# An embedding, attention and mixture-of-experts kernel on one core: V fetched in smaller pieces and partly later, first score loads ahead of a meeting, experts' tokens in three groups instead of five

## What is computed

```python
def _L0_attn_ref(x, w_qkv, b_qkv, w_proj, b_proj):
    y = x @ fq_weight(w_qkv).T + b_qkv
    y, _ = fq_act(y)                       # 8 bits, one scale for all of q, k and v
    q, k, v = ...                          # 64 sequences of 68 tokens, 12 heads of 16
    attn = jnp.einsum('bhnd,bhmd->bhnm', q, k) * attn_scale
    attn, s_attn = fq_act(attn)            # one scale for all scores
    attn = int_log_softmax(attn, s_attn)
    o = jnp.einsum('bhnm,bhmd->bhnd', attn, v)
    o, _ = fq_act(o)
    o = o @ fq_weight(w_proj).T + b_proj
    o, _ = fq_act(o)
    return o

def _L0_ffn_ref(x, w_fc_sh, w_proj_sh, w1, w2, router_w, balance_bias):
    shared = _mlp(x, w_fc_sh, w_proj_sh)
    scores = jax.nn.sigmoid(xf.astype(jnp.float32) @ router_w.T)
    _, idx = jax.lax.top_k(scores + balance_bias, K)        # 2 of 8 experts
    tw = jnp.take_along_axis(scores, idx, axis=-1)
    tw = tw / (tw.sum(-1, keepdims=True) + 1e-20)
    ...
    return shared + routed.reshape(Bx, Tx, Cx)

h = concatenate(patches of the images @ W, text embedding MLP)   # 64 x 68 tokens, 192 wide
h = h + _L0_attn_ref(_layernorm(h), ...)
h = h + _L0_ffn_ref(_layernorm(h), ...)
```

## Time and profile before

| What | Value |
|---|---|
| median of 3 runs | 942.96 us (940.64 to 943.77) |
| the profiled execution's own time | 945.13 us |
| its span | 943.2 us |
| DVE, PE, ACT, POOL busy | 709.8, 604.6, 515.3, 252.1 us |
| mean granted TensorE clock | 0.709 |
| DMA | 92.77 MB, mean 98 GB/s |

### The profile page before, as it was taken

One profiled execution on the slowest core, in us unless ns is written; L12 is line 12 of the kernel. 1 busy time (PEld: TensorE's weight loads), 2 busy tenths in 40 slices (PEclk: granted clock), 3 DMA queues, 4 the chain that ended last, 5 costly groups with the idle time before them and its releaser, 6 DMA issues.

```text
span 943.2 us, 19819 instructions
## 1 busy us (share of the span) xinstructions
PE 604.6 (64%) x6474; PEld 451.9 (48%) x6474; DVE 709.8 (75%) x1831; ACT 515.3 (55%) x951; POOL 252.1 (27%) x245
## 2 busy tenths in 40 slices
PE   3589889898406667058888888341222349999970
PEld 2589768776204334024555555331112237777760
DVE  2535668777548999789999999987776788667783
ACT  3122268766345424048888888454554226888840
POOL 2022111120011221012222222110355750036575
PEclk9999789999755555555565555555555569999985
DMA  7974024443222221022222222451011241467753
GB/s 172 258 202 120 18 54 131 109 119 120 96 66 82 68 68 51 9 47 33 43 43 43 43 43 37 106 220 59 33 55 58 77 147 51 140 188 218 226 168 113
DMA packets 151481, 92.77 MB, mean 98 GB/s; under 512 B 88828, under 2 KB 143684, under 8 KB 151084
## 3 DMA queue, kind: packets, MB, share of 16 engines
q1 hardware_dynamic: 143560, 72.28, 29.3%
q0 software_dynamic: 7856, 19.68, 7.2%
HBM read 45.62 MB, written 31.85 MB: 82 GB/s over the span
## 4 chain that ended last, share of the span: by engine, by line
DVE 28%; PE 24%; issue 17%; SPq 16%; ACT 9%; DMA 3%; POOL 2%; POOLq 0%; DVEq 0%; ACTq 0%
PE ps L1844 19%; SPq L659 8%; ACT R L806 5%; ACT R L809 3%; DVE M L1413 3%; DVE M L1414 3%; SPq L637 2%; POOL R L799 2%; SPq L636 2%; SPq L638 2%; DVE R L1403 2%; DVE R L1801 1%; PE ps L2018 1%; PE ps L2114 1%; PE ps L1869 1%
## 5 line engine op out<-in xcount | busy, mean ns | idle before, releaser
L1844 PE MATMUL ps<-R 128*128 128x256 f16 (+9 forms) x2064 | 310.2, 303 | 53.0 <-DVE R L1801 16.1
L1844 PEld LDWEIGHTS ps<-R 128*128 128x128 f16 (+5 forms) x2064 | 221.6, 129 | 113.3 <-issue 59.1
L806 ACT ACTIVATE R<-ps 128x768 f16<-128x768 f16 (+7 forms) x257 | 159.8, 649 | 93.5 <-PE ps L2018 18.9
L1844 PE MATMUL ps<-M 32*128 32x68 bf16 (+4 forms) x1196 | 100.6, 242 | 117.5 <-DMA M<-R 67.2
L1844 PEld LDWEIGHTS ps<-M 32*128 32x128 bf16 (+3 forms) x1196 | 64.9, 115 | 168.9 <-issue 66.5
L809 ACT ACTIVATE R<-R,sc 128x512 f16<-128x512 f32 (+7 forms) x107 | 83.6, 838 | 105.6 <-DVE R L1403 40.1
L799 POOL DMA_INDIRECT R<-y_by_tile,M x68 | 66.7, 981 | 98.0 <-DMA y_by_tile<-R 79.4
L771 POOL TENSOR_TENSOR R<-R,M 128x884 f32<-128x884 f32 x32 | 53.2, 1664 | 145.5 <-ACT M L958 145.5
L790 POOL DMA_INDIRECT x_by_expert<-R,M x68 | 67.2, 989 | 60.3 <-DVEq L1707 40.5
L806 ACT ACTIVATE R<-R 128x512 f16<-128x512 f32 (+4 forms) x121 | 64.1, 549 | 35.3 <-DVE R L1801 34.5
L2018 PE MATMUL ps<-ident_b,R 128*68 128x128 bf16 x416 | 53.8, 298 | 25.3 <-ACT R L806 23.9
(11 more groups left out here) (293 smaller groups left out, 1050.2 us busy)
## 6 DMA issues: line engine op xcount, KB each, us to landing
R<-x_by_expert SPq DMA_DIRECT2D x41, 192.0 KB, 2.6
y_by_tile<-R SPq DMA_DIRECT2D x41, 192.0 KB, 2.3
R<-in_x_dram SPq DMA_DIRECT2D x12, 576.0 KB, 9.0
M<-R SPq DMA_DIRECT2D x16, 260.0 KB, 2.3
M<-R SPq DMA_DIRECT2D x32, 130.0 KB, 2.0
R<-w_split SPq DMA_DIRECT2D x1, 4032.0 KB, 23.1
R<-h_rows SPq DMA_DIRECT2D x1, 3264.0 KB, 14.3
out_dram<-R SPq DMA_DIRECT2D x17, 192.0 KB
```

The costliest lines, as they stand in the source:

```text
L806: return act.activation(out_, in_, ACT.Copy)
L1844: return pe.matmul(o, a, b, start=start, stop=stop, skip_group_check=True)
```

## The change

Four groups of edits:

1. **V.** `V_LOADS` keeps only sequences 6 to 32, in five pieces of 4 or 6 sequences; the loads of 32 to 48 and 0 to 6 at step 26 and of 48 to 64 at the end are gone from SP's list. Ten pieces (`V_LATE`) are issued by ACT after the meeting, two after each of the chunks 1 to 5. The rounding of V into `VQ` moves from DVE to POOL, in the list ahead of POOL's reduction of the score extremes; `spread_v` waits for it by a new semaphore.
2. **Constants.** Five DVE instructions (`output_constants`) move from just ahead of the second meeting to chunk 1 of the first pass.
3. **Ahead of a meeting.** `barrier` takes a function that is called between the engine's sign-in and its wait: SP issues the staging loads of groups 0 and 1 and PE the scores of group 0 there at the second meeting; SP issues `load_rest` there at the third.
4. **Experts.** Windows of 5, 7 and 5 pairs instead of 2, 4, 5, 4, 2; `SHARED_FIRST` 10 instead of 12; `READY` becomes 17, 31, 41; combines 1.5 steps apart instead of 2. DVE normalises (`normal`) instead of ACT; the root is `Sqrt` and the score `Sigmoid` instead of `Ln` and `Exp`; `weigh` is part of `choose` again; the order of DVE's and ACT's lists is regular.

```diff
-WINDOWS = [(0, 2), (2, 6), (6, 11), (11, 15), (15, 17)]
-SHARED_FIRST = 12
+WINDOWS = [(0, 5), (5, 12), (12, 17)]
+SHARED_FIRST = 10
-        def barrier(eng, name):
+        def barrier(eng, name, ahead=None):
             eng.drain().then_inc(sem("all_engines_done"), 1)
+            if ahead:
+                ahead()
             eng.wait_ge(sem("all_engines_done"), 5 * n)
-        V_LOADS = [(20, 11, 24, 32), (24, 12, 6, 24), (26, 6, 32, 48), (26, 6, 0, 6), (None, 15, 48, B)]
+        V_LOADS = [(20, 11, 24, 28), (20, 11, 28, 32), (24, 12, 6, 12), (24, 12, 12, 18), (24, 12, 18, 24)]
+        V_LATE = [(1, 0, 4), (1, 4, 6), (2, 32, 36), (2, 36, 40), (3, 40, 44), (3, 44, 48), (4, 48, 52), (4, 52, 56), (5, 56, 60), (6, 60, B)]
-            COMBINE_AT.append(max(free, COMBINE_AT[-1] + 2 if i else 0))
+            COMBINE_AT.append(max(free, COMBINE_AT[-1] + 1.5 if i else 0))
...
-            sp.wait_ge(sem("qkv_extremes"), 16)
-            load_v(48, B, 15)
+                sp.wait_ge(sem(f"v_saved{a}"), v_stores(16 + a))
+                sp.wait_ge(sem(f"w_stored{a}"), 16 * sum(WCH_DMAS[a::2]))
...
+            def load_ahead():
+                for g in range(2):
+                    wait(sp, "scored", 32 + g - 1)
+                    load_seqs(g, slice(g * 2, g * 2 + 2), 2)
-            barrier(sp, "sp")
+            barrier(sp, "sp", load_ahead)
...
-            pipeline(sp, [(load_two, 0), (spread_v, 4), (load_rest, 4)], 32)
-            barrier(sp, "sp")
+            pipeline(sp, [(load_two, 0), (spread_v, 4)], 32)
+            barrier(sp, "sp", load_rest)
...
+            pool.wait_ge(sem("v_added"), 2)
+            pool.tensor_scalar(VQ, vt, sc[0:N, Q_CAPM:Q_CAPM + 1], H16 + 512.0, ALU.min, ALU.subtract).then_inc(sem("v_whole"), 1)
             reduce_pair(A_MX, "a_minmax")
...
             for c in range(8):
                 to_halves(c)
+                for at, first, end in V_LATE:
+                    if c == at:
+                        act.dma_start(yv[:, first:end, :], v_dram[:, first:end, :]).then_inc(sem("v_in"), 16)
...
-                chain(act, "scalar_step", act.activation(rs2[:, 1, t], rs2[:, 0, t], ACT.Ln))
-                act.activation(rs2[:, 1, t], rs2[:, 1, t], ACT.Exp, scale=0.5).then_inc(sem("ln2_sqrt"), 1)
+                act.activation(rs2[:, 1, t], rs2[:, 0, t], ACT.Sqrt).then_inc(sem("ln2_sqrt"), 1)
...
+            def output_constants():
+                for k, (lo, hi) in enumerate(((C1, C1 + 3), (C1 + 1, P), (C1 + 2, P))):
+                    ch(dve.tensor_reduce(bmask[:, k:k + 1], ident[:, lo:hi], X, ALU.add, negate=k > 0))
+                ch(dve.reciprocal(vrow, prow))
+                ch(tt(bprow, bprow, vrow, ALU.mult))
...
-            dve.wait_ge(sem("v_added"), 2)
-            ts(VQ, vt, s1(Q_CAPM, N), H16 + 512.0, ALU.min, ALU.subtract)
...
+            def normal(i):
+                wait(dve, "rows2", i - 1)
+                for j in range(2):
+                    n = 2 * i + j
+                    last = ts(xf[:, i % 2, j, :], hf[:, n, :], mv2[:, n, 0:1], rs2[:, 2, n:n + 1], ALU.subtract, ALU.mult)
+                last.then_inc(sem("xf"), 1)
...
+            residuals(0, 5)
             variances(0)
+            residuals(5, 7)
             deviations(0)
+            normals(0)
+            residuals(7, 9)
             choose(0)
+            residuals(9, 11)
             place(0)
+            residuals(11, 12)
             variances(1)
...
+            def scores_ahead():
+                pe.wait_ge(sem("st_qk0"), 9 * 48)
+                pe.wait_ge(sem("extremes"), 31)
+                scores(0, 0, 0, 0, 1)
...
-            barrier(pe, "pe")
+            barrier(pe, "pe", scores_ahead)
```

More of the change, by code:

```diff
@@ L614, in _ @@
                     if s == at:
-                        if end == 48:
-                            for a in range(2):
-                                sp.wait_ge(sem(f"w_stored{a}"), 16 * sum(WCH_DMAS[a::2]))
-                        if first == 0:
-                            sp.wait_ge(sem("h_out"), 16 + 4 * GRID)
-                        load_v(first, end, UNIT_ORDER.index(unit) if unit < 15 else 15)
+                        load_v(first, end, UNIT_ORDER.index(unit))
                 if s - 2 in WSTEP:
@@ L1731, in make_table @@
                 ch(dve.memset(step_[:, 0, :], float(WB)))
[L1732 removed]
+                for w in range(3):
                     last = dve.memset(step_[:, 0, E * (w + 1) - 1:E * (w + 1)], -float((E - 1) * WB))
@@ L2099, in turn_window @@
                         route(i - 2)
-            for w in range(NW):
+            for w in range(3):
                 turn_window(w)
```

210 lines of the change are left out of this document (73 added, 137 removed).

## The result

The changed kernel takes **967.68 us** (median of 4 runs, 967.10 to 969.18) against 943.37 us (4 runs, 940.64 to 947.03) for the kernel before: a ratio of 1.0258 (1.0221 to 1.0295). It is slower by 24 us; I had forecast 16 us faster. The profiled execution of after took 969.18 us, its span is 967.4 us. Times are medians of a kernel's fast executions; one slow execution of e10 (2485 us) and one of e12 (1358 us) are left out.

What follows compares the result with a forecast made beforehand. Bounds: DVE's wait behind V fetches, its chain at the second meeting, SP's release at the third, POOL's indirect DMAs last. Terms -12.5 + 1.0 + 1.9 - 2.5 - 4.5 - 1.3 + 0.9 = -17.0 gave 928.1 or 926.0; forecast 927 us, range 918 to 938.

Steps and rivals of the forecast that it cites:

- It reads one tensor, so I take the copy: POOL's rounding of V: priced at a copy's 1.12 ns per element, 13.8 us; bounds memset 11.0, two-tensor product 23.1.
- V, rounded by POOL: Ahead of POOL's reduction at the second meeting: moving the rounding from DVE costs +1.9 us, ends -0.9 and +11.2.
- My rule for the point from which it decides: Second meeting: POOL's pass, started at 371.74, sets the reduction's start once it takes over 8.5 us.
- V, in the first pass: Ten late V pieces beside SP's staging copies: +1.0 us, bounds 0 to +3.8.
- The wait at the first meeting: End of the qkv stage: V fetches ahead of the stores make DVE's wait; moving them saves 12.5 us, bounds 0 to 12.5.
- Constants and scores ahead: Second meeting: constants moved into the first pass -2.5 us, first loads and scores issued before the meeting -4.5.
- the third meeting: POOL's reduction there no longer waits for SP's issuing: -1.3 us.
- Tiles and the longer run of gathers: Experts, first store to last gather: 31 tiles for the second group +5.3, 48 gathers instead of 44 +5.1, together +10.4 us.
- the combines' +1.5: Experts' end: combines 1.5 steps apart make DVE wait for gathers at each window's end, +1.5 us (0 to 3).
- The first store: Experts: the first tile's store moves from 803.31 to 792.3, -11.0 us, after earlier rows and PE's lowered clock.
- the first scatter: Experts: first window's rows ready at 680 instead of 666.12, about 14 us later; last scatter about 2 earlier.
- The rival on the other side: POOL's pass eats every gain from 30.8 us (2.5 ns per element) on; kernel slower, 943 to 950 us; chance 0.04.

Runs made afterwards that it cites:

- e10: e3's kernel with all the experts' edits taken back (five groups, ScalarE normalises): 999.48 us beside 993.83 for e3's kernel on the same chip.
- e12: e3's kernel with four groups of tokens instead of three and combines 2 steps apart: 981.40 us beside 993.83 for e3's kernel on the same chip.
- e2: Changed kernel with eight POOL probe instructions (68 x 1536 elements each) in place of its pass, VectorE rounding V; copy 1.46 us, pass's own form 5.47 and 5.45.
- e8: e3's kernel with VectorE's rounding of V replaced by a plain POOL copy, clipping and shift left out: 1003.33 us, ratio 0.9762 to before.
- e3: Changed kernel with V rounded by VectorE again and each late V piece fetched as rows 0 to 63 and 64 to 67: 920.34 us, ratio 0.9734 to before.
- e5: Changed kernel with VectorE rounding V and the five early V loads of before, none late, each split into 64 and 4 rows: 1001.70 us, ratio 0.9743.
- e7: e3's kernel with first loads and scores, constants and y-part loads back in their places behind the meetings: 1005.77 us, ratio 0.9788 to before.
- e16: Changed kernel, POOL's pass kept, with only its ten late V pieces split into rows 0 to 63 and 64 to 67: 1035.78 us, ratio 1.0107.
- e9: Repeat of e3's kernel, unchanged, on a chip where before takes 1025 to 1028 us: 993.83 us, ratio 0.9707 to before.

## Why the prediction was wrong

**The step that failed: "It reads one tensor, so I take the copy".** The term "V, rounded by POOL" was +1.9 and is +35.9. I priced an instruction that isn't in the trace by the number of tensors it reads, 1.12 ns per element, with a product's 1.88 ns as the upper end. e2 shows that on POOL the form sets the price, and not the number of tensors read: 0.95 for a copy, 2.0 for two tensors, 2.7 and 3.6 for a scalar operation with one and two steps. My two rates lie near what e2 has for a copy and for two tensors; the form of the pass was in none of my rows. The pass of before on VectorE, 3.42 us in the earlier trace rows, is twelve times cheaper. My rule for the point from which it decides (371.74 + p against 383.64) was right: with p = 41.65 and the 6.01 us, it gives 419.4, +35.8. The Trainium skill's tight loop (GPSIMD Engine Reference, section 3.1), 1.5 ns by my estimate, is also less than half of the measured 3.4 ns; its advice to leave elementwise work on VectorE is what held.

**A part that was missing from the step: the 6 us ahead of the reduction.** Nothing in before's trace showed them, since POOL always stood idle for long ahead of a reduction. With a copy in the pass's place, the form that I had priced, the term is +4.5 (e8), though the copy took 10.4 us and not my 13.8. So even there my +1.9 was too low.

**The second term mis-sized: "V, in the first pass", +1.0 and measured +8.6.** I had reasoned that pieces from another issuing engine's queue pass the staging copies by, and had capped it at 3.8 us since only the first pieces met a wait. But queues of two issuing engines are not apart: each pair of pieces takes some 5.1 us (2 x 204 KB at 82 GB/s) on what looks like a quarter of the DMA engines, and SP's last copy for a half chunk, which lands after 5.7 us in place of 2.0, then sets PE's start. The first scores came 2.5 us later, counted from DVE's last scaling of V, and each of the next two chunks took 3.0 us more; the single pieces cost next to nothing. So the cost came with all the pairs, and my cap counted only the first. I had read the share of 0.24 in the earlier trace rows and taken it as a rate to compute with; its meaning, that three quarters of the engines had nothing to do, was what I missed. e3 and e5 show that the shape is the cause: split rows remove the late pieces' cost, and most of the wait. That the wait is gone by moving the fetches was right as forecast; that it was the fetches' shape the prediction didn't see.

**What held.** The wait at the first meeting was the fetches' (-12.5 forecast, -12.0). Constants and scores ahead: -7.0 and -7.0; the third meeting: -1.3 and -0.8; e7 has them together as 8.3. Tiles and the longer run of gathers +10.4 and +10.6; only the combines' +1.5 did not come. The first store, -11.0 and -11.2, came out by two errors that cancel: counted from the y part's reduction the first scatter came 14.2 us later (forecast 14), but the last 0.6 us earlier and not 2.4, so that the first turn moved by 12.6 us and not 13.9, and from there to the store, with PE at the lower clock at first, it took 1.4 us more and not 2.8. That agreement is luck in part.

**The rival on the other side** named the mechanism, with its threshold of 30.8 us, and had 0.04, and even its 943 to 950 us was too low: the bounds came from rows that had nothing of its kind. With the rest as forecast, 41.65 + 6.01 would have given 961; the 7.6 us more of the first pass make 968.5, and 967.7 was measured.

What stays open: why three groups are 5 us better than five on one kind of chip, while the two traces have them equal on the other; what POOL does in the 6 us; and which of step and scalar makes its scalar operations dear.

## What to carry to other kernels

An instruction moved to another engine has no price until one of its own form, with its arithmetic steps, has been seen on that engine; bound it by the dearest class and not by the number of tensors, and ask what stands behind it in that engine's list (here a reduction, on which every engine waits). When a stretch shows a DMA share near 0.25 with bytes waiting, look at the shape of the transfer before its place in the queue: 64 + 4 rows gave, with nothing moved, most of what the ten late pieces give when they are split too. And where groups hand work on from one queue to another, add up for each group the release and the run behind it: the largest of these sums ends the kernel, and one more group took 12 to 15 us off.

## What the runs showed of the hardware

- POOL, 68 x 1536 elements: copy 1.46 us, memset 1.37, two tensors 3.08, scalar with one step 4.09, with two steps 5.46; VectorE needs 3.42 us for eight times as many with two steps.
- A reduction over partitions starts 5.9 to 6.0 us after a scalar operation or a copy of POOL that ends right ahead of it (after 6.01, e2 5.95, e8 5.89, e16 5.96), and within 0.3 us of DVE's last result where POOL had been idle for 23 us.
- A fetch of 68 rows moves 82 GB/s on a share of 0.24 to 0.25 of the DMA engines; as 64 and 4 rows the stretch has 0.69 and 153 GB/s, stores included. Beside pairs of late pieces of 68 rows a copy of 34 KB from another engine's queue lands after 5.7 us (before 2.0).
- Between chips: on three of them before takes 1025 to 1028 us instead of 944. In the trace of e9 ScalarE waits 45.1 us for what the profile calls "remote" between 655 and 780 us, and PE 34.8 us in 22 waits on "issue", beside POOL's scatters; on the first kind of chip this stretch has no such rows among its longest waits.
